# A reordered single-core program: attention and a mixture of experts with new tables of steps, and gate before weight in an expert step

## The chip, the core and the metric

The program runs on one core of one Trainium2 chip. The time is the device time of one execution in microseconds; three runs of the kernel before gave 528.85, 529.96 and 534.11, median 529.96. Engines are named as in the profile: PE is TensorE, ACT ScalarE, DVE VectorE, POOL GpSimd, SP SyncE.

## The reference, cut to what matters

```python
xn = layernorm(x)                                   # x: 4 batches x 1024 tokens x 128
q, k, v = heads(xn @ w_qkv + b_qkv)                 # 16 heads of 8
ctx_g = attend(q[:, :4], k[:, :4], v[:, :4], causal)            # 4 global heads
ctx_l = attend(q[:, 4:], k[:, 4:], v[:, 4:], causal, window 32) # 12 local heads
s = ctx @ w_out + b_out
scores = sigmoid(xn @ gate_w.T)                     # 16 experts, top 2 of 4 groups, top 4 of these
cw = 2.5 * topk_w / topk_w.sum()                    # weight of each expert for each token
y = sum_e cw_e * (silu(xn @ Wg_e.T) * (xn @ Wu_e.T)) @ Wd_e.T + shared expert
out = x + s * silu(xn + y)
```

## The kernel before

Batches are worked on one after the other, in chunks (c = 0, 1) of 512 tokens. The 16 heads form four groups of four: three local groups (g = 0, 1, 2) and the global one (g = 3). One hand-made list of steps per section gives the order of everything: FIRST (before batch 0), BODY (three times, for batches 0 to 2) and LAST (batch 3). A letter of a table takes the next step of a stream: R the attention run, A its operands, X expert steps, P, T and V the preparation, routing and values of the *next* batch, C the context, 0 and 1 the outputs, I the setup. BODY ends with the first six expert steps of the next batch. Every engine walks the same list and does its own part of each step, in that order and with no reordering; semaphores tie the parts together.

The steps that the text names:
- `ln c`, `xT c`, `gate`, `q c`, `k c`: layer norm, transposed x, routing logits (its result `th`, ACT line 926), queries and keys. `q` and `k` are each split into a high and a low part, the low one (`qkl`) by POOL (line 1235); SP then writes both to planes in DRAM.
- `route 0` to `route 6`: choice of experts, small VectorE operations (line 964 and others), which ends with `cw`; `cwT c` transposes it.
- `weights k lo hi`: transposes of expert weights on PE; ACT makes `up_hi` and VectorE `up_lo` for k = 0, 1.
- `strips g`, `pads g half`, `kpads g`: SP's loads of a head group from the planes (2, 4 and 4 DMAs, lines 526, 536 and 546). They wait until the operands that they overwrite have been used; `strips 1` waits until `qfull 0 0` has been copied out of its bank by ACT.
- `max g n`: a product of queries and keys whose row maxima VectorE takes (line 1176, local groups 1178); `maxdone` spreads them (POOL, `maxd`, line 1245), `qfull g c` subtracts them on PE, and ACT copies the result to `qall` (line 929). Group 3 has 48 maximum tiles; `max 3 0` is the first to use the group's strips and pads.
- `score g n`, `pv g n`: scores (ACT takes the exponential, line 936) and their product with the values. `norm`, `fold`, `ctx`, `proj`, `mul`, `outT` end a batch.
- `up c t`: an expert step for a pair of experts (t = 8 the shared one): a tile of the experts' weights (1 matmul, `wrow`), gate and up tiles (3 each). ACT: tanh of the gate (854), a copy `gates` (859) that waits for POOL's multiplication of the step before, and `wrow` (865). POOL multiplies `wrow` (1253); `times c t` multiplies on VectorE (1140) and POOL (1262); `down c t` is the last product.

PSUM has 8 banks. Attention tiles take banks 0 to 2 in turn, expert tiles (and those of preparation) 3 to 5; 6 and 7 are accumulators. A tile waits until its bank's last user has emptied it. `Section.__init__` (line 225) gives out the banks in the list's order.

Of the kernel before, what the change touches and what calls it, by code (L numbers as in the profile page):

```python
# [43 lines left out]
EP = E // 2  # L44
# [97 lines left out]
def expert_steps(c):  # L142
    out = []
    for t in range(NUP + LAG_DOWN):
# [4 lines left out]
        if t >= LAG_DOWN:  # L149
# [1 line left out]
    return out  # L151


FIRST_ORDER = ("IPIPIPPIPIITTPIIPTTTPPVITTPIVIITTIXXXXIVPPPVPPVXXVPXXIXPVPPVXPXXVVXXX")
BODY_ORDER = ("AAXRRAXXAXPARRAXAXRAXAAAAARPRRAXAAAAAAAXAAXRRAARARAARRRRARAAAAAAAAAAAAARAXARAXRRXRPAXRAXAAAARRRA"
              "AARAAAARAXRRARRARRAAAARXARRRRXARAPAARRXRARRRRXRAAPRAXAAXRARXRRRRRARRARRAAPPARXAXRRRPXRRCRRRXXRRR"
              "RRPRTRRPRXRRRRXRRXRTRRRRPXRRTPTXRRXRTXRRRRXXXRRRPRRRRCTRXRRRRRRRRRRRRPTRPXXRXPPPXRRRTRRRPTRXCXVX"
              "CV00XVXVV1X1VXVPV0XXVXV1XXXXX")
LAST_ORDER = ("AXAXARRRXAXARXXRAAAAAAAXAAARAARRRAARXARAARAAAARRRAAXARRAAAAAAAAAAXAAAXAAARXRRRARAXRAAARARRAAAAAA"
              "RXXARARARXRARARARRRAARARAAARARAXAAXAAXARARXAXAARRARRRRRRRRRXRRRRRRXRAAXRRXRXRXRRRXRRRRRCRRRRRXRX"  # L160
              "RCRRRRRXRRRRRRRRRRRRRRRRRRXRXRRRRRXRRRRRRRRRRRRRRRRRRXXRXXCXCXX0X0X1011")
# [42 lines left out]
def batch_steps(more):  # L204
# [14 lines left out]
class Section:  # L219
# [5 lines left out]
    def __init__(self, steps):  # L225
        self.steps, self.place = steps, {}
        self.fills, self.empties = [0] * BANKS, [0] * BANKS
        turns = {ATT: 0, EXP: 0}
        for s in steps:
            if s[0] == "down" and s[2] == 0:  # L230
                self.place[("y", s[1])] = (Y, self.fills[Y], self.empties[Y])
            if s[0] == "z":
                self.add(("z", s[1]), Y, 0)
            if s[0] == "pv" and s[2] == 0:
                self.add(("acc", s[1], 0), ACC, 0)
            if s == ("pv", GLOBAL, CUT):
                self.add(("acc", GLOBAL, 1), ACC, 0)
            if s[0] in ("pv", "down", "norm", "qpads", "z", "z2", "ln", "stats", "pads", "kpads", "maxdone", "ctx", "route", "times",
                        "mul", "strips", "setup", "fill", "ones"):
                continue  # L240
            ahead = s[0] == "max" and s[1] == 0
            ring = EXP if s[0] in ("up", "weights", "xT", "q", "k", "gate") or ahead else ATT
            parts = [s] if s[0] != "up" else [s + (x,) for x in ("weight", "gate", "up") if x != "weight" or s[2] < EP]
            for part in parts:
                self.add(part, ring[turns[ring] % len(ring)], 1)
                turns[ring] += 1
# [45 lines left out]
def build(nc, x, w_qkv, b_qkv, w_out, b_out, gate_w, gate_bias, Wg, Wu, Wd, Ws_g, Ws_u, Ws_d,  # L292
          c32, c16, out):
    with ExitStack() as ctx:
# [109 lines left out]
        k32_loaded = sem("k32_loaded")  # L404
# [156 lines left out]
        def _(pe):  # L561
# [25 lines left out]
            def walk(at):  # L587
                b, opened = at.b, set()
                for s in at.steps:
# [6 lines left out]
                            ins = pe.transpose(ps[:, P * (i - s[2]):P * (i - s[2] + 1)], stage[:, s[1], i, :], ident)  # L596
                        done(at, s, ins)
                    elif kind == "small":
                        pe.wait_ge(k32_loaded, 16)
                        pe.wait_ge(small_loaded, 5 * 16)  # L600
                        pe.wait_ge(small_ready, 1)
                        ps = fill(at, s)
# [166 lines left out]
                    elif kind == "up":  # L769
# [23 lines left out]
                    elif kind == "outT":  # L793
# [551 lines left out]
```

## Time and profile before

| | |
|---|---|
| runs | 528.85, 529.96, 534.11 us |
| the profiled execution | 530.82 us, of it the span 529.0 us |
| granted clock, mean | 0.981 |
| PE / PEld busy | 480.5 us (91%) / 289.0 (55%) |
| DVE / ACT / POOL busy | 340.3 (64%) / 330.3 (62%) / 265.9 us (50%) |
| DMA | 32.37 MB, mean 61 GB/s |

First steps: batch 0 starts (`qfull 0 0` on PE) at 57.72 us, batch 1 at 179.60, batch 2 at 301.92, batch 3 at 421.51. Busy time is the time in which an engine has an instruction in work; PE's instructions overlap, so that its busy time holds small gaps. A busy share is a mean over stages with different limits, so the stages are looked at one by one below. The granted clock is TensorE's: 1.0 is 2.4 GHz, 0.5 is 1.2 GHz.

### The profile page before, as it was taken

How to read it: one execution, taken by the hardware profiler on the slowest of the kernel's cores; microseconds unless marked ns; L12 is line 12 of the kernel's file. 1: busy time of each engine (PE TensorE's matmuls, PEld its weight loads, DVE VectorE, ACT ScalarE, POOL GpSimd, SP SyncE). 2: the span in 40 equal slices, each digit the busy share in tenths (PEclk: the TensorE clock that was granted, in tenths of full speed). 3: DMA queues.
4: the chain of work that ended last, by engine and by line, in shares of the span. 5: the costliest groups of instructions: out<-in, count | busy, mean ns of one | idle time of the engine just before them, and what ended most of it. 6: DMA issues, size and time to landing. Idle time of an engine off the chain costs nothing.

```text
span 529.0 us, 10545 instructions
## 1 busy us (share of the span) xinstructions
PE 480.5 (91%) x3804; PEld 289.0 (55%) x3832; DVE 340.3 (64%) x755; ACT 330.3 (62%) x654; POOL 265.9 (50%) x239
## 2 busy tenths in 40 slices
PE   1969988999999988999999998999999987989995
PEld 0756655555457655555446765555456755544442
DVE  6876464885687555777588474877588532686415
ACT  3456744767957544666957546566967556266972
POOL 3227851265736952155745972155744962016623
PEclk9979998999999999999999999999999999899999
DMA  9256383000350575000360396000260187000001
GB/s 216 80 164 115 58 103 64 1 1 2 124 76 0 165 96 82 1 1 1 93 109 0 91 162 89 2 0 1 82 119 2 48 156 97 2 2 0 1 1 40
DMA packets 144077, 32.37 MB, mean 61 GB/s; under 512 B 120966, under 2 KB 136346, under 8 KB 144026
## 3 DMA queue, kind: packets, MB, share of 16 engines
q1 hardware_dynamic: 143696, 31.41, 30.2%
q8 instruction: 30, 0.49, 0.4%
q10 hardware_dynamic: 330, 0.30, 0.3%
q14 instruction: 21, 0.17, 0.1%
HBM read 22.25 MB, written 9.44 MB: 60 GB/s over the span
## 4 chain that ended last, share of the span: by engine, by line
PE 72%; DVE 9%; ACT 6%; issue 6%; SPq 2%; POOL 2%; DMA 1%; POOLq 1%; DVEq 0%; ACTq 0%
PE bank L791 10%; PE bank L739 7%; PE bank L678 6%; PE bank L572 6%; PE bank L574 6%; PE bank L573 6%; PE bank L708 5%; DVE mxp L1176 4%; PE bank L755 4%; PE bank L779 3%; ACT stage L936 2%; PE bank L690 2%; PE bank L720 2%; PE bank L646 2%; PE bank L662 1%
## 5 line engine op out<-in xcount | busy, mean ns | idle before, releaser
L936 ACT ACTIVATE stage<-bank 128x512 f32<-128x512 f32 (+3 forms) x240 | 112.5, 528 | 62.0 <-PE bank L720 32.2
L1253 POOL TENSOR_TENSOR wrow<-wrow,gates 128x512 f32<-128x512 f32 x64 | 82.1, 1283 | 97.1 <-ACT wrow L865 96.9
L1176 DVE TENSOR_REDUCE mxp<-bank 128x1 f32<-128x512 f32 (+4 forms) x192 | 90.3, 518 | 41.1 <-PE bank L681 32.8
L1262 POOL TENSOR_TENSOR hid<-hid,wrow 128x512 f32<-128x512 f32 x64 | 81.8, 1278 | 37.1 <-DVE hid L1140 31.9
L1140 DVE SCALAR_TENSOR_TENSOR hid<-hid,bank 128x512 f32<-128x512 f32 x72 | 48.7, 680 | 60.0 <-PE bank L574 39.9
L791 PE MATMUL bank<-hid,down_w 128*128 128x512 f32 x144 | 77.8, 629 | 0.0
L854 ACT ACTIVATE hid<-bank 128x512 f32<-128x512 f32 x72 | 43.3, 602 | 51.1 <-PE bank L574 50.9
L1245 POOL TENSOR_TENSOR maxd<-mxp,k 128x512 f16<-128x512 f32 x32 | 33.4, 1048 | 79.7 <-DVE mxp L1176 45.7
L678 PE MATMUL bank<-kall,qpad 128*128 128x512 f16 (+4 forms) x192 | 54.0, 331 | 12.6 <-issue 6.8
L572 PE MATMUL bank<-xh,up_hi 128*128 128x512 f32 x144 | 58.3, 405 | 0.0
L708 PE MATMUL bank<-kpad,kall 128*128 128x512 f16 (+3 forms) x192 | 55.3, 330 | 2.0 <-ACT stage L936 0.6
L574 PE MATMUL bank<-xl,up_hi 128*128 128x512 f32 x144 | 56.7, 394 | 0.0
L573 PE MATMUL bank<-xh,up_lo 128*128 128x512 f32 x144 | 56.5, 392 | 0.0
L1178 DVE TENSOR_REDUCE mxp<-bank 128x8 f32<-128x512 f32 x48 | 31.8, 687 | 23.8 <-PE bank L690 23.4
L708 PEld LDWEIGHTS bank<-kpad,kall 128*128 128x128 f16 x192 | 18.0, 97 | 51.7 <-issue 24.1
L859 ACT ACTIVATE gates<-bank 128x512 f32<-128x512 f32 x72 | 43.2, 600 | 1.6 <-POOL wrow L1253 1.3
L739 PE MATMUL bank<-stage,vg 128*32 128x512 f32 (+3 forms) x384 | 40.5, 498 | 0.0
L678 PEld LDWEIGHTS bank<-kall,qpad 128*128 128x128 f16 x192 | 17.2, 98 | 42.7 <-DVE mxp L1176 23.5
L865 ACT ACTIVATE wrow<-bank 128x512 f32<-128x512 f32 x64 | 39.1, 610 | 0.0
L779 PE MATMUL bank<-cwT,pairsel 128*128 128x512 f32 x64 | 33.7, 526 | 0.8 <-ACT wrow L865 0.7
L572 PEld LDWEIGHTS bank<-xh,up_hi 128*128 128x128 f32 x144 | 27.3, 189 | 9.6 <-issue 3.8
L1123 DVE RECIPROCAL denT<-denT 128x256 f32<-128x256 f32 x16 | 27.8, 1745 | 5.1 <-ACT ctxT L893 5.1
(158 smaller groups left out, 884.4 us busy)
## 6 DMA issues: line engine op xcount, KB each, us to landing
planes<-qkh SPq DMA_DIRECT2D x16, 256.0 KB, 3.1
qtmp<-planes SPq DMA_DIRECT2D x16, 256.0 KB, 3.2
kall<-planes SPq DMA_DIRECT2D x16, 256.0 KB, 3.5
qpad<-planes SPq DMA_DIRECT2D x128, 32.0 KB, 2.9
kpad<-planes SPq DMA_DIRECT2D x48, 64.0 KB, 3.3
xin<-in_L_attn_x_dram SPq DMA_DIRECT2D x4, 512.0 KB, 4.6
planes<-qkl SPq DMA_DIRECT2D x8, 256.0 KB, 3.0
xres<-in_L_attn_x_dram SPq DMA_DIRECT2D x4, 512.0 KB, 4.1
```

Of the source, the lines that this page charges most:

```text
L572: pe.matmul(ps[:], w_hi, x_hi, start=True, stop=False)
L573: pe.matmul(ps[:], w_lo, x_hi, start=False, stop=False)
L574: return pe.matmul(ps[:], w_hi, x_lo, start=False, stop=True)
L678: ins = pe.matmul(ps[:, 0:cols], qpad[:, j, :, :], kall[:, g % 2, CH * c:CH * c + cols], start=True, stop=not last, skip_group_check=True)
L708: ins = pe.matmul(ps[:, 0:cols], kall[:, g % 2, P * j:P * (j + 1)], kpad[:, g % 2, q0 // BLK:(q0 + cols) // BLK, h, :], start=True, stop=n ...
L739: ins = pe.matmul(acc[BLK * h:BLK * (h + 1), q0 - CH * c:q0 - CH * c + cols], vg[:, j, h, :], prob[:, (SCORES_BEFORE[g] + m) % NPROB, 0:cols],
L779: done(at, s + (x,), pe.matmul(ps[:], pairsel[:, t, :], cwT[:, chunk(c)], start=True, stop=True))
L791: pe.matmul(banks[Y][:], down_w[:, t, :], hid[:, i % NHID, :], start=(t == 0), stop=(t == NUP - 1)).then_inc(down_done, 1)
L936: act.activation(prob[:, t % NPROB, 0:cols], ps[:, 0:cols], ACT.Exp).then_inc(freed, 1)
L1176: ins = dve.tensor_reduce(mxp[:, c, j:j + 1], ps[:, 0:cols], AX_X, ALU.max)
L1253: pool.tensor_tensor(row, row, gates[:], ALU.mult).then_inc(gated, 1)
L1262: pool.tensor_tensor(hid[:, i % NHID, :], hid[:, i % NHID, :], wrow[:, (EP * c + t) % NWT, :] if t < EP else gates[:], ALU.mult)\
```

## The change

Three edits. The tables FIRST_ORDER, BODY_ORDER and LAST_ORDER have new values; each holds the same letters as before, so the same steps are done. In an expert step other than the first, the tiles are made in the order gate, weight, up instead of weight, gate, up, and get their banks in that order. TensorE's wait for the 32-bit constants stands at its head instead of in step `small`.

```diff
-FIRST_ORDER = ("IPIPIPPIPIITTPIIPTTTPPVITTPIVIITTIXXXXIVPPPVPPVXXVPXXIXPVPPVXPXXVVXXX")
+FIRST_ORDER = ("PPIPPIPIIPPTITIPITTIIIITTIVPTPVTTPXXVVVXXVIXIVPXPXIXXPVPPPPPVPXVXXXXX")
...
-            parts = [s] if s[0] != "up" else [s + (x,) for x in ("weight", "gate", "up") if x != "weight" or s[2] < EP]
+            parts = [s] if s[0] != "up" else [s + (x,) for x in ("gate", "weight", "up") if x != "weight" or s[2] < EP]
...
                     elif kind == "small":
-                        pe.wait_ge(k32_loaded, 16)
...
-                        for x in ("gate", "up", "weight") if first else ("weight", "gate", "up"):
+                        for x in ("gate", "up", "weight") if first else ("gate", "weight", "up"):
...
+            pe.wait_ge(k32_loaded, 16)
             sections(pe, walk)
```

SP's instructions stand in the same order as before. Lines behind 599 are one lower in the new kernel, up to line 799.

ScalarE (ACT) at the start of the program, before: the constants' setup (lines 819 to 826), both copies of `xT`, then the first `up_hi` and `th`.

```order
L819 ACT_TABLE_LOAD
L819 ACTIVATE kbf<-k 128x128
L822 ACTIVATE kbf<-k 128x448
L823 ACTIVATE kbf<-k 128x64
L822 ACTIVATE kbf<-k 128x448
L823 ACTIVATE kbf<-k 128x64
L824 ACTIVATE repeat<-k 128x512
L826 ACTIVATE pairsel<-k 128x1024
L915 ACTIVATE xT<-bank 128x512 x2
L840 ACTIVATE up_hi<-bank 128x512 x2
L926 ACTIVATE th<-bank 128x128
```

And now:

```order
L915 ACT_TABLE_LOAD
L915 ACTIVATE xT<-bank 128x512
L819 ACTIVATE kbf<-k 128x128
L822 ACTIVATE kbf<-k 128x448
L823 ACTIVATE kbf<-k 128x64
L822 ACTIVATE kbf<-k 128x448
L823 ACTIVATE kbf<-k 128x64
L824 ACTIVATE repeat<-k 128x512
L826 ACTIVATE pairsel<-k 128x1024
L915 ACTIVATE xT<-bank 128x512
L926 ACTIVATE th<-bank 128x128
```

The setup has moved behind the first copy of `xT`, and `q 0` (lines 923 and 924) ahead of the first `up_hi`.

VectorE in the second half of routing, before (`need` and `pre` are route 4, `gt` to `cw` routes 5 and 6):

```order
L964 TENSOR_TENSOR eq<-msk,top 128x128
L964 TENSOR_TENSOR pre<-msk,top 128x8x16
L1029 TENSOR_REDUCE need<-gt 128x8
L964 TENSOR_TENSOR pre<-pre 128x8x16 x4
L964 TENSOR_TENSOR pre<-pre,need 128x8x16
L967 TENSOR_SCALAR pre<-pre 128x8x16
L964 TENSOR_TENSOR eq<-eq,pre 128x128
L964 TENSOR_TENSOR vn_lo<-bank,vn_hi 128x384
L964 TENSOR_TENSOR up_lo<-bank,up_hi 128x512
L964 TENSOR_TENSOR gt<-gt,eq 128x128
L964 TENSOR_TENSOR msk<-sc,gt 128x128
L1046 TENSOR_REDUCE need<-msk 128x8
```

And now:

```order
L964 TENSOR_TENSOR eq<-msk,top 128x128
L964 TENSOR_TENSOR pre<-msk,top 128x8x16
L964 TENSOR_TENSOR up_lo<-bank,up_hi 128x512 x2
L964 TENSOR_TENSOR up_lo<-bank,up_hi 128x128
L1029 TENSOR_REDUCE need<-gt 128x8
L964 TENSOR_TENSOR pre<-pre 128x8x16 x4
L964 TENSOR_TENSOR pre<-pre,need 128x8x16
L967 TENSOR_SCALAR pre<-pre 128x8x16
L964 TENSOR_TENSOR eq<-eq,pre 128x128
L964 TENSOR_TENSOR gt<-gt,eq 128x128
L964 TENSOR_TENSOR msk<-sc,gt 128x128
L1046 TENSOR_REDUCE need<-msk 128x8
```

Two large `up_lo` and a small one stand ahead of route 4, where one large one stood ahead of route 5; `vn_lo` has moved behind route 5.

POOL from the third expert step of the first stage on, before (1253 and 1262 are the two multiplications of a step, `causal` and `foldsel` setup):

```order
L1253 TENSOR_TENSOR wrow<-wrow,gates 128x512
L1262 TENSOR_TENSOR hid<-hid,wrow 128x512
L1245 TENSOR_TENSOR maxd<-mxp,k 128x512
L1253 TENSOR_TENSOR wrow<-wrow,gates 128x512
L1208 MEMSET causal 32x32
L1208 MEMSET causal 32x64
L1208 MEMSET causal 32x96
L1213 CAST causal<-k 32x32 x4
L1217 COPY foldsel<-k 128x32 x2
L1262 TENSOR_TENSOR hid<-hid,wrow 128x512
L1253 TENSOR_TENSOR wrow<-wrow,gates 128x512
L1245 TENSOR_TENSOR maxd<-mxp,k 128x512
```

And now:

```order
L1253 TENSOR_TENSOR wrow<-wrow,gates 128x512
L1262 TENSOR_TENSOR hid<-hid,wrow 128x512
L1253 TENSOR_TENSOR wrow<-wrow,gates 128x512
L1208 MEMSET causal 32x32
L1208 MEMSET causal 32x64
L1208 MEMSET causal 32x96
L1213 CAST causal<-k 32x32 x4
L1217 COPY foldsel<-k 128x32 x2
L1262 TENSOR_TENSOR hid<-hid,wrow 128x512
L1245 TENSOR_TENSOR maxd<-mxp,k 128x512 x2
L1253 TENSOR_TENSOR wrow<-wrow,gates 128x512
```

Both `maxd` of group 0 stand together, ahead of the fifth `wrow`; before, the first stood ahead of the fourth `wrow` and the second behind the fifth.

TensorE in BODY, from `max 3 12` (416 columns) on, before; 791 is `down`, 715 and 720 a score of group 2:

```order
L678 MATMUL bank<-kall,qpad 128x416
L681 MATMUL bank<-kbf 128x32
L678 MATMUL bank<-kall,qpad 128x448
L681 MATMUL bank<-kbf 128x32
L791 MATMUL bank<-hid,down_w 128x512
L678 MATMUL bank<-kall,qpad 128x480
L681 MATMUL bank<-kbf 128x32
L715 MATMUL bank<-kbf 128x512
L720 MATMUL bank<-qall,kpad 128x64 x8
L678 MATMUL bank<-kall,qpad 128x512
L681 MATMUL bank<-kbf 128x32
L791 MATMUL bank<-hid,down_w 128x512
```

And now:

```order
L677 MATMUL bank<-kall,qpad 128x416
L680 MATMUL bank<-kbf 128x32
L790 MATMUL bank<-hid,down_w 128x512
L677 MATMUL bank<-kall,qpad 128x448
L680 MATMUL bank<-kbf 128x32
L677 MATMUL bank<-kall,qpad 128x480
L680 MATMUL bank<-kbf 128x32
L677 MATMUL bank<-kall,qpad 128x512
L680 MATMUL bank<-kbf 128x32
L790 MATMUL bank<-hid,down_w 128x512
L714 MATMUL bank<-kbf 128x512
```

`down 0 7` stands one tile earlier, and the score between the last two maxima has gone to the other three behind `down 0 8`.

## Rows read from the trace of the kernel before

**Rows 1.** Stretches: us, PE, PEld, DVE, ACT, POOL busy (count), clock, DMA, GB/s.
```profile
0.00:57.72 57.72, 39.27 (x191) 31.13 (x194) 40.85 (x116) 28.47 (x51) 25.63 (x36) 0.94 0.55 132
57.72:85.11 27.39, 23.48 (x321) 15.98 (x324) 13.14 (x37) 16.65 (x31) 17.02 (x15) 1.00 0.69 105
85.11:93.75 8.64, 8.35 (x74) 4.34 (x75) 7.46 (x21) 2.59 (x6) 1.05 (x1) 0.80 0.09 9
...
179.60:206.92 27.32, 23.31 (x321) 16.07 (x324) 12.99 (x37) 15.93 (x30) 15.32 (x13) 1.00 0.81 141
206.92:216.04 9.12, 8.82 (x73) 4.33 (x75) 7.37 (x21) 2.54 (x6) 1.05 (x1) 0.81 0.08 9
216.04:242.38 26.34, 25.28 (x222) 14.35 (x221) 21.50 (x44) 17.80 (x39) 12.05 (x10) 1.00 0.00 1
242.38:281.99 39.61, 39.21 (x240) 19.88 (x240) 27.34 (x66) 30.46 (x63) 20.16 (x18) 1.00 0.32 68
...
301.92:327.54 25.62, 23.34 (x322) 16.01 (x325) 13.01 (x37) 15.45 (x29) 15.33 (x13) 1.00 0.83 148
327.54:335.64 8.10, 7.67 (x74) 3.95 (x75) 7.37 (x21) 2.89 (x7) 1.05 (x1) 1.00 0.13 14
...
449.41:486.92 37.51, 34.66 (x288) 18.25 (x289) 27.88 (x59) 17.84 (x38) 11.92 (x10) 0.95 0.01 2
```

**Rows 2.** Timeline of SyncE's queue, batch 1: start us, us, line, operation.
```profile
180.90 0.34 SPq L526 DMA_DIRECT2D qtmp<-planes  x1
...
197.13 4.02 SPq L546 DMA_DIRECT2D kpad<-planes  x4
...
202.37 4.36 SPq L536 DMA_DIRECT2D qpad<-planes  x8
```

**Rows 3.** Timeline of TensorE, batch 1; in brackets the idle time before, releaser.
```profile
206.92 0.18 PE L678 MATMUL bank<-kall,qpad 128*128 128x32 f16 x1 [1.45 <-issue]
```

**Rows 4.** Timeline of VectorE, first stage.
```profile
4.42 1.76 DVE L1105 MEMSET kpad<- 128x2048 uint32 x1 [0.38 <-issue]
...
33.39 0.68 DVE L964 TENSOR_TENSOR up_lo<-bank,up_hi 128x512 fp32r<-128x512 f32 x1
...
35.79 0.29 DVE L1053 SCALAR_TENSOR_TENSOR cw<-msk,wsum 128x128 f32<-128x128 f32 x1
...
44.39 1.28 DVE L1178 TENSOR_REDUCE mxp<-bank 128x8 f32<-128x512 f32 x2
```

**Rows 5.** The view of the line that loads the first x.
```profile
DMA to landing us min/median/max: 4.7/4.7/4.7
```

**Rows 6.** Timeline of ScalarE, first stage.
```profile
4.50 0.31 ACT L819 ACTIVATE kbf<-k 128x128 bf16<-128x128 f32 x1
...
6.46 1.04 ACT L826 ACTIVATE pairsel<-k 128x1024 fp32r<-128x1024 f32 x1
13.71 0.60 ACT L915 ACTIVATE xT<-bank 128x512 f32<-128x512 f32 x1 [6.20 <-PE bank L614]
...
19.89 0.28 ACT L926 ACTIVATE th<-bank 128x128 f32<-128x128 f32 x1 [2.63 <-PE bank L646]
```

**Rows 7.** VectorE's additions of routing: count, ns min/median/max, first and last start us.
```profile
L964 DVE TENSOR_TENSOR pre<-pre x4: 281/292/1153, 29.7 to 30.8; 128x128 f32<-128x128 f32 x4
...
L964 DVE TENSOR_TENSOR msk<-msk,gm x1: 1278/1278/1278, 26.5 to 26.5; 128x128 f32<-128x128 f32 x1
```

**Rows 8.** Timeline of POOL, first stage.
```profile
30.67 1.15 POOL L1235 TENSOR_TENSOR qkl<-sT,qkh 128x512 f16<-128x512 f32 x1 [1.77 <-ACT qkh L924]
40.82 1.29 POOL L1253 TENSOR_TENSOR wrow<-wrow,gates 128x512 f32<-128x512 f32 x1 [9.00 <-ACT wrow L865]
...
47.86 1.29 POOL L1253 TENSOR_TENSOR wrow<-wrow,gates 128x512 f32<-128x512 f32 x1 [1.44 <-ACT wrow L865]
...
56.72 1.26 POOL L1253 TENSOR_TENSOR wrow<-wrow,gates 128x512 f32<-128x512 f32 x1
```

**Rows 9.** Timeline of SyncE's queue, the first strips of batch 0.
```profile
59.66 0.34 SPq L526 DMA_DIRECT2D qtmp<-planes  x1
```

More of the change, by code:

```diff
@@ L151, in expert_steps @@
     return out
-FIRST_ORDER = ("IPIPIPPIPIITTPIIPTTTPPVITTPIVIITTIXXXXIVPPPVPPVXXVPXXIXPVPPVXPXXVVXXX")
[L155 to L161, printed above, removed]
+FIRST_ORDER = ("PPIPPIPIIPPTITIPITTIIIITTIVPTPVTTPXXVVVXXVIXIVPXPXIXXPVPPPPPVPXVXXXXX")
+BODY_ORDER = ("AAAXRRRXAPRXXXAAAAAAAXRXAAARARPRAAXAAAAARXAXRRRRRAAAAARRRAAAAAAAARAAAAAAXAAAXRRRRXAPRAXXAAAARRRA"
+              "AAAARAAXRRARARARRRARAAAXXRARRRARRAPRAAXARRRRRXRRAAPAXAAXRRRRRXAAARRRRRRAAXRAPPAXRRPRXRRRXRXRTRRR"
+              "RRPRRTPRRRRRXRRTXRRRXXRPRRRRXRXRRRRRPPTRCTRXTXRRRRXRXCRRPRXTPRRRRPPRRRRRRRRXRXXPRRRRRXRTTRPCXXVX"
+              "V0XVC0VXVXVXV1V1VXXP0X1VXXXXX")
+LAST_ORDER = ("AAXXARRRRRAXAXXAARRXAARAAAARAXAXAAARRARAARRXAAAARARRAAAAAAAAAAAAAAXAAAXARAXRRRAAXARARRARARRAAAAA"
+              "RXAXARAARARARARRRRAARRAAAARXAAXARAXARXARAXAAAXAARRRRRRRXRRRXRRRRRRRRAAXRXRXRRXRRRRXXRRRRRRRRRRRX"
+              "RCRRRXRRRRRRCRRRRXRRRRRRRRXRRRRRRXRRXRRRRRRRRRRRRRRRRRXRXXX0XCCX0X1X011")
 FIRST_EXPERTS = expert_steps(0) + [("z", 0), ("z2", 0)]
```

## The prediction

> **What bounds the kernel now.** I read the page's busy shares, then the table by stretches [rows 1], then SyncE's and TensorE's timelines, then the start of the program on every engine. Batch 1 stands for batches 0 to 2; the marks are the first TensorE instruction of a step. The reader is to see four kinds of stretch in [rows 1].
>
> From the first query-bias tile of a batch to the first global maximum tile (`max 3 0`): 27.39 us in batch 0, 27.32 in batch 1, 25.62 in batch 2. TensorE has about 23.3 of work there. SyncE is what ends it: it issues strips, pads and k pads of three head groups without a pause, from 180.90 to beyond 202.37 [rows 2], and `max 3 0`, which needs the first half of the third group's pads, starts at 206.92 after 1.45 us of waiting for nothing but a transfer [rows 3]. The length of this stretch is that of 34 issues, counted from the first, `strips 1`: 30 of them took the 21.5 us between these two rows.
>
> Then 9.12 us (batch 1) or 8.10 (batch 2) to the batch's step `up 1 0`. The granted clock is 0.81 in one and 1.00 in the other: TensorE is at 1.2 GHz for part of the first, after the waits above.
>
> Then 26.34 us up to the routing logits (`gate`), with VectorE 21.50 busy, since 32 maximum tiles and four `times` go through it: VectorE and its hand-overs bound it. In the last batch this and the stretch before it together take 37.51 us, VectorE 27.88 busy.
>
> Then 39.61 us with TensorE 39.21 busy: only TensorE bounds it, and no order of the same steps shortens it. The first stage, 57.72 us with TensorE 39.27 busy, is a chain over VectorE and POOL (below).
>
> **The change, part by part.** No instruction's size changes. What moves is which waits are covered.
>
> *Waits and the order in a step.* The wait for the 32-bit constants moves to TensorE's head; they are used later anyway, so 0. Gate before weight: TensorE makes the gate tile one matmul earlier in a step and asks for the bank of the previous gate, which ScalarE gives back before the weight's. TensorE is 39.21 of 39.61 busy where steps are dense, so this is worth 0 there; in the first stage it is inside the next sum.
>
> *Batch starts.* SyncE's rows stay the same, word for word. Its 34 issues start when `qfull 0 0` has been evacuated, and that step stays first. So moving scores, downs and maxima within this stretch changes how much TensorE waits and not where `max 3 0` starts: 0, three times and in the last batch. If SyncE had to wait for a later maximum, it would cost; the nearest, the first half of pads 2 behind `max 1 1`, keeps its place in BODY.
>
> *From `max 3 0` to `up 1 0`.* `down 0 7` moves ahead of `max 3 13`, and the four scores of group 2 stand together. VectorE is 7.37 of 9.12 busy, so at most 1.7 per batch is there to gain. A score no longer waits between two maxima; I take 0.4, nearer to nothing, since all maxima keep their place: 3 x 0.4 = -1.2 for batches 0 to 2 and 0 for the last; ends 0 and -5.1.
>
> *From `up 1 0` to `gate`.* VectorE idles 4.84 of 26.34 in each body batch, and 9.63 of 37.51 in the last. Scores, `times` and `pv` change places by one to three steps, the maxima hardly. I take 0, with ends of 1.5 us per batch either way, a third of that idle time.
>
> *The first stage.* Here real things move.
> 1. VectorE's memset of `kpad` (1.76, [rows 4]) leaves the place ahead of the statistics. x is issued at 0.73 and lands 4.7 later [rows 5], so they start near 5.5 instead of 6.1, when that memset is over: -0.6. But it now stands between the two halves of the layer norm, and the second half ends 1.76 + 0.38 - 0.6 = 1.5 later, near 15.
> 2. ScalarE's setup of constants, seven activations from 4.50 to 7.50 [rows 6], ran while x was loaded. Now it stands between the copies of `xT 0` (its end, 14.31 before, is 0.6 earlier) and `xT 1`: 13.7 + 3.0 + 0.6 = 17.3. `gate` needs both and starts near 18.0, so `th` is at 21.4 instead of 19.89 [rows 6]: +1.5.
> 3. Routing on VectorE took 19.89 to 36.08, 16.2 us [rows 4, 6]. The change puts two more large `up_lo` into it, 2 x 0.68 [rows 4], and ScalarE evacuates `q 0` ahead of the first `up_hi` that VectorE then waits for, about 1.1. Two routing operations of about 0.29 took 1.28 and 1.15 [rows 7], the second exactly beside POOL's `qkl` of 30.67 to 31.82 [rows 8]. POOL now has `q 0` and `k 0` early and `q 1` and `k 1` only after routing's longest parts, so I take off both stretches, 0.99 + 0.86. Routing ends at 21.4 + 16.2 + 1.4 + 1.1 - 1.85 = 38.25: +2.2.
> 4. From there to POOL's first `wrow` it is 40.82 - 36.08 = 4.74 [rows 4, 8]; so that starts at 43.0.
> 5. POOL then runs to the end of its fifth `wrow`, 57.98, in 17.16 us, with 1.44 idle [rows 8]. The idle time goes, since it starts later; a second `maxd` (1.04) comes ahead of this `wrow`. 43.0 + 17.16 - 1.44 + 1.04 = 59.8: +1.8. ScalarE's `gates` of the sixth step waits for it, and the copy of `qfull 0 0` stands behind that; so `strips 1` is issued near 61.5 to 61.7 instead of 59.66 [rows 9]: **+2.0**.
>
> What is late next: `k 1` ends on POOL near 41, not at 31.8 [rows 8]. The first maximum was reduced 12.6 later, at 44.39 [rows 4], so now near 53.7; POOL reaches its `maxd` near 56.7, so 3 us are left. Ends of this term: 0 (the two later parts absorbed by POOL and TensorE) and +3.9.
>
> Whose stretch it was: VectorE's addition took 1.15 while POOL read two inputs, 0.29 otherwise, in one and the same line [rows 7]. The Trainium skill (SBUF — State Buffer, "Who interferes with whom") says that a VectorE instruction with two SBUF inputs and a GpSimd instruction that reads SBUF exclude each other for a whole instruction. The trace agrees. By that rule the 1.85 goes, as taken; without it, with the stretches kept, the sum is 1.85 higher.
>
> **Sum.** The profiled execution took 530.82 us (span 529.0 and 1.8 around it). 530.82 + 2.0 - 1.2 = 531.6. It lies 0.86 above the median of the runs, 529.96; on that scale the forecast is **530.8 us**.
>
> **Rivals.**
> *Slower: VectorE's stretch loses.* Place: `up 1 0` to `gate`, four times. For it: the same 26.3 us three times over [rows 1], so whatever the order does there it does in each batch; more scores stand directly behind one another in the ring of three banks that the maxima use too. Against it: VectorE's work is the same 21.5. Price: 1.5 x 4 = 6 us, 536.8. It decides from 1.1 us per batch.
> *Faster: the same stretch gains.* `times 1 0` now fills VectorE while TensorE makes two scores. Price 1.6 x 4 = 6.4, 524.4.
> *Batches start as batch 2 does.* It needed 25.62 + 8.10 = 33.72 against 36.44 in batch 1 and 36.03 in batch 0: shorter k-pad issues (4.02 in batch 1, [rows 2]) and no low clock. The table of orders does not move these issues, so it would be luck: -2.7 -2.3 and as much in the last batch, minus what is forecast, near 524.5.
> *The first stage loses nothing:* POOL and TensorE take up the 2.0: 528.8.
> *The stretches stay* (the page's rule is not what lengthened them, or another POOL operation lands there): 532.6.
> *The change does nothing it says:* if transfers were not what the order was short of, times stay at 529 to 531; this is within the forecast.
>
> **Numbers.** Chances: forecast 0.45, stretches stay 0.10, first stage loses nothing 0.12, slower 0.16, faster stretch 0.12, starts as batch 2 0.05. A measurement of this kernel tells about 1%, 5.3 us, from no change. Below 524.7 lie the two faster cases, 0.17; above 535.3 the slower one, 0.16; between them 0.67. The range leaves out the far halves of both: 523.5 to 537.0. The forecast's own range is 528.5 to 533.5.
>
> **What would show it.** Right: `th` near 21.4, the routing weights `cw` near 38.3, POOL's first `wrow` near 43.0, `strips 1` near 61.6; SyncE without gaps from there and `max 3 0` about 25.5 us behind it; VectorE near 21.5 busy in 26.3 us from `up 1 0` to `gate`. Wrong: `cw` at 36 or at 41; a wait of SyncE inside its 34 issues; a stretch to `gate` of less than 25.2 or more than 27.4; another number of stretches with granted clock 0.8.

## The result, and the profile after

Twenty runs of the changed kernel gave a median of 533.75 us (530.96 to 539.28), twenty of the kernel before 530.99 us (525.70 to 534.11). The ratio is 1.007, 95% interval 1.0047 to 1.0092: about 3.7 us slower by the ratio, 2.8 us by the medians. That is within the range on record (523.5 to 537.0), 3 us above the forecast of 530.8 and just outside the forecast's own range (528.5 to 533.5). The forecast was a loss of 0.8 us, so the size of the change was missed by a factor of some four.

The profiled execution of the changed kernel took 530.96 us (span 529.2), the lowest of its twenty, while that of before, 530.82, was a middling one. So the two spans are nearly equal, and the loss has to be looked for in stretches. The table by stretches, columns as in [rows 1] (a stretch, length, then busy us and count of PE, PEld, DVE, ACT and POOL, granted clock, DMA share, GB/s):

```profile
0.00:62.62 62.62, 38.31 (x192) 30.06 (x194) 40.43 (x116) 28.82 (x53) 28.06 (x38) 0.92 0.51 121
62.62:88.75 26.13, 22.86 (x321) 15.87 (x324) 12.08 (x37) 14.29 (x27) 14.65 (x13) 1.00 0.72 110
88.75:96.66 7.91, 7.54 (x73) 3.99 (x75) 7.39 (x20) 3.62 (x8) 1.05 (x1) 1.00 0.13 13
182.54:208.41 25.87, 22.84 (x321) 15.87 (x324) 12.34 (x37) 14.58 (x28) 15.30 (x13) 1.00 0.84 144
208.41:216.32 7.91, 7.55 (x73) 3.99 (x75) 7.39 (x20) 3.72 (x8) 1.05 (x1) 1.00 0.13 13
216.32:242.65 26.33, 24.85 (x221) 14.54 (x220) 20.86 (x44) 17.39 (x38) 12.70 (x10) 1.00 0.01 2
302.19:328.64 26.45, 22.83 (x321) 15.88 (x324) 12.06 (x37) 15.57 (x29) 15.31 (x13) 1.00 0.83 143
328.64:336.55 7.91, 7.55 (x74) 4.00 (x75) 7.40 (x20) 2.74 (x7) 1.05 (x1) 1.00 0.15 15
450.18:487.91 37.73, 35.30 (x292) 19.06 (x294) 28.23 (x59) 19.91 (x43) 12.30 (x10) 0.95 0.02 3
```

The first row is 62.62 us long against 57.72 in [rows 1]: 4.9 us lost before batch 0 starts. Later starts lie closer: `qfull 0 0` of batch 1 at 182.54 (179.60 before), of batch 2 at 302.19 (301.92), of batch 3 at 422.69 (421.51). This execution was a lucky one there: from the first of these starts to the last it took 360.1 us, and four other kernels with the same batches (they differ from the changed one in the first table alone) took 363.5 to 367.3. The stretch from `max 3 0` to `up 1 0` is 7.91 us three times, with granted clock 1.00, where [rows 1] show 8.64 and 9.12 at 0.80 and 0.81, and 8.10 at 1.00. Beside the passage of 8.10, at the same clock, the new order gains 0.2. The low clock is not the old table's doing: body_last_new (below) has the new BODY table and took 8.74 us at 0.80 in batch 0, and a_old_first, which has it too, shows a granted clock of 0.81 from 83.2 to 92.0 us. The stretch behind `up 1 0` (26.33 against 26.34, VectorE 20.86 busy against 21.50) is unchanged; it ends here just behind the last maximum tile, since the new table puts `gate` 3.4 us later.

The first stage in rows that answer to [rows 4], [rows 6] and [rows 9], of ScalarE, VectorE and SyncE's queue (start and length in us; in brackets the idle time before and what ended it):

```profile
21.90 0.28 ACT L926 ACTIVATE th<-bank 128x128 f32<-128x128 f32 x1 [4.55 <-PE bank L645]
...
39.25 0.29 DVE L1053 SCALAR_TENSOR_TENSOR cw<-msk,wsum 128x128 f32<-128x128 f32 x1
...
54.63 0.69 DVE L1178 TENSOR_REDUCE mxp<-bank 128x8 f32<-128x512 f32 x1 [2.19 <-PE bank L689]
...
63.91 0.34 SPq L526 DMA_DIRECT2D qtmp<-planes  x1
```

POOL's row, which answers to [rows 8], dense from its first `wrow` on but for 0.43 us ahead of the fifth:

```profile
44.23 1.30 POOL L1253 TENSOR_TENSOR wrow<-wrow,gates 128x512 f32<-128x512 f32 x1 [1.94 <-ACT wrow L865]
...
59.92 1.30 POOL L1253 TENSOR_TENSOR wrow<-wrow,gates 128x512 f32<-128x512 f32 x1 [0.43 <-ACT wrow L865]
```

`th` is 2.0 later than before, `cw` 3.5, POOL's first `wrow` 3.4, `strips 1` 4.25. The chain of waits of the same stretch (start, us, what) goes another way than through POOL's row, through the pads and TensorE:

```profile
39.98 1.17 POOL qkl L1235
41.16 0.52 SPq L517
...
44.31 4.47 DMA planes<-qkl
48.80 0.34 SPq L526
...
53.55 2.35 DMA qpad<-planes
55.91 0.05 issue
55.96 0.39 PE bank L683
```

And TensorE waits for these pads in front of the first maxima; in brackets idle time and releaser:

```profile
51.49 1.02 PE L790 MATMUL bank<-hid,down_w 128*128 128x512 f32 x2
54.20 0.39 PE L689 MATMUL bank<-kall,qpad 128*128 128x32 f16 x8 [1.70 <-DMA qpad<-planes]
...
55.96 0.39 PE L683 MATMUL bank<-kbf 128*128 128x512 bf16 x1 [0.47 <-DMA qpad<-planes]
```

The reader is to see two ways that meet near 60 us: routing, `cw`, POOL's row of multiplications; and `k 1`, planes, strips, pads, maxima, then the fifth and sixth expert step on TensorE. In this execution the second came last. ScalarE's copy of `qfull 0 0`, which `strips 1` waits for, had been waiting for TensorE, with POOL's fifth `wrow` over at 61.22:

```profile
63.24 1.08 ACT L929 ACTIVATE qall<-bank 128x512 f16<-128x512 f32 x2 [0.64 <-PE bank L662]
```

### The profile page after: what moved, and what is told of

The parts are those of the page before. It is cut to its first block, busy times and chain, and to the rows that moved or that the text cites. A ratio compares the mean times of both kernels' runs of the same rounds, so it can differ in the third digit from the quotient of the medians.

```text
span 529.2 us, 10542 instructions
## 1 busy us (share of the span) xinstructions
PE 474.1 (90%) x3805; PEld 287.0 (54%) x3832; DVE 339.9 (64%) x755; ACT 328.5 (62%) x654; POOL 267.4 (51%) x239
## 4 chain that ended last, share of the span: by engine, by line
PE 72%; DVE 6%; SPq 6%; issue 5%; ACT 5%; DMA 4%; POOL 1%; DVEq 1%; POOLq 0%; ACTq 0%
PE bank L790 10%; PE bank L738 7%; PE bank L572 7%; PE bank L707 6%; PE bank L574 6%; PE bank L573 6%; PE bank L677 5%; PE bank L754 4%; DVE mxp L1176 4%; SPq L536 3%; PE bank L778 2%; PE bank L689 2%; ACT stage L936 2%; PE bank L719 2%; DMA kall<-planes 2%
## 5 line engine op out<-in xcount | busy, mean ns | idle before, releaser
L790 PE MATMUL bank<-hid,down_w 128*128 128x512 f32 x144 | 76.7, 618 | 0.0
L572 PE MATMUL bank<-xh,up_hi 128*128 128x512 f32 x144 | 66.4, 461 | 0.4 <-DVE hid L1140 0.3
L677 PE MATMUL bank<-kall,qpad 128*128 128x512 f16 (+4 forms) x192 | 51.8, 321 | 10.7 <-issue 3.5
L738 PE MATMUL bank<-stage,vg 128*32 128x512 f32 (+3 forms) x384 | 39.4, 496 | 0.0
L1235 POOL TENSOR_TENSOR qkl<-sT,qkh 128x512 f16<-128x512 f32 x16 | 18.9, 1182 | 38.0 <-ACT qkh L924 38.0
L929 ACT ACTIVATE qall<-bank 128x512 f16<-128x512 f32 x32 | 18.1, 596 | 23.4 <-PE bank L662 23.4
```

The costliest lines, as they stand in the source:

```text
L572: pe.matmul(ps[:], w_hi, x_hi, start=True, stop=False)
L677: ins = pe.matmul(ps[:, 0:cols], qpad[:, j, :, :], kall[:, g % 2, CH * c:CH * c + cols], start=True, stop=not last, skip_group_check=True)
L738: ins = pe.matmul(acc[BLK * h:BLK * (h + 1), q0 - CH * c:q0 - CH * c + cols], vg[:, j, h, :], prob[:, (SCORES_BEFORE[g] + m) % NPROB, 0:cols],
L790: pe.matmul(banks[Y][:], down_w[:, t, :], hid[:, i % NHID, :], start=(t == 0), stop=(t == NUP - 1)).then_inc(down_done, 1)
```

## The experiments

Each ratio is to the kernel before, with its 95% interval; "strips 1" and "max 3 0" are starts in batch 0 of the profiled execution, one for each kernel.

| kernel | median us | ratio | strips 1 | max 3 0 |
|---|---|---|---|---|
| before | 530.99 | 1 | 59.66 | 85.11 |
| changed | 533.75 | 1.007 (1.0047 to 1.0092) | 63.91 | 88.75 |
| first_new | 533.83 | 1.006 (1.0027 to 1.0093) | 63.23 | 88.13 |
| gate_first | 528.60 | 0.9952 (0.9922 to 0.9981) | 57.89 | 83.13 |
| body_last_new | 530.22 | 0.9999 (0.9966 to 1.0032) | 58.86 | 83.40 |
| a_old_first | 530.07 | 1.0006 (0.9978 to 1.0035) | 57.92 | 83.24 |
| a_weight_first | 536.28 | 1.0098 (1.0064 to 1.0132) | 64.43 | 89.07 |
| a_k1_early | 532.75 | 1.0057 (1.0027 to 1.0088) | 64.15 | 89.23 |
| a_setup_early | 534.48 | 1.0072 (1.0042 to 1.0103) | 62.93 | 88.32 |
| a_warm | 533.64 | 1.0059 (1.0028 to 1.009) | 63.30 | 88.58 |
| a_warm_k1 | 532.93 | 1.0054 (1.0025 to 1.0084) | 61.63 | 87.11 |
| kpads_late | 524.30 | 0.989 (0.9845 to 0.9935) | 58.84 | 82.96 |
| kp_gate | 521.38 | 0.9846 (0.9807 to 0.9885) | 57.91 | 82.08 |
| best | 519.70 | 0.9801 (0.9762 to 0.984) | 57.79 | 80.43 |

### The parts of the change, one at a time

**first_new**, the kernel before with the new first table and the moved wait of TensorE:

```diff
-FIRST_ORDER = ("IPIPIPPIPIITTPIIPTTTPPVITTPIVIITTIXXXXIVPPPVPPVXXVPXXIXPVPPVXPXXVVXXX")
+FIRST_ORDER = ("PPIPPIPIIPPTITIPITTIIIITTIVPTPVTTPXXVVVXXVIXIVPXPXIXXPVPPPPPVPXVXXXXX")
...
-                        pe.wait_ge(k32_loaded, 16)
...
+            pe.wait_ge(k32_loaded, 16)
```

> The kernel before with the new FIRST_ORDER alone (and the wait for the 32-bit constants at TensorE's head); BODY, LAST and the order of tiles as before. Theory A (the whole loss of the change is made in the first stage and the start of batch 0, through the later k 1, the planes and the first maxima): strips 1 issued near 63.9 instead of 59.66 us, max 3 0 of batch 0 between 88.5 and 89.5 instead of 85.11, and the time 3 to 4.5 us above the kernel before, since nothing behind it gives anything back. Rival B (the first stage's loss is absorbed later and BODY and LAST cost what the change costs): within 1 us of the kernel before.

Measured 1.006, 3.2 us: the whole loss, as theory A had it. `strips 1` came at 63.23 and `max 3 0` at 88.13, each a little earlier than it said.

**gate_first**, the kernel before with the order of tiles alone:

```diff
-            parts = [s] if s[0] != "up" else [s + (x,) for x in ("weight", "gate", "up") if x != "weight" or s[2] < EP]
+            parts = [s] if s[0] != "up" else [s + (x,) for x in ("gate", "weight", "up") if x != "weight" or s[2] < EP]
...
-                        for x in ("gate", "up", "weight") if first else ("weight", "gate", "up"):
+                        for x in ("gate", "up", "weight") if first else ("gate", "weight", "up"):
```

> The kernel before with the one change of the order gate, weight, up in an expert step, in its banks too. All tables as before. Theory A: 0, within 0.7 us of the kernel before, since TensorE is 39.2 of 39.6 us busy where steps are dense and elsewhere SyncE or VectorE sets the end. Rival B: the weight tile, one matmul later in each step, makes ScalarE's wrow and POOL's multiplication later, and the DVE-bound stretches from up 1 0 to gate lengthen from 26.3 to some 27 us: 2 to 3 us slower.

Neither: 2.5 us faster (interval 1.0 to 4.1 of 530). In the first stage it is about 1 us: `strips 1` at 57.89 against 58.86 and 58.84 in the two profiles with the same first table and weight first (59.66 in the kernel before). POOL waited 0.54 us for its third `wrow` where it had waited 1.44, and 1.42 in body_last_new. From `qfull 0 0` of batch 0 to that of the last batch it took 364.7 us, no less than before (363.8), so the trace places no more than that 1 us.

**body_last_new**, the kernel before with the other two tables:

```diff
-BODY_ORDER = ("AAXRRAXXAXPARRAXAXRAXAAAAARPRRAXAAAAAAAXAAXRRAARARAARRRRARAAAAAAAAAAAAARAXARAXRRXRPAXRAXAAAARRRA"
+BODY_ORDER = ("AAAXRRRXAPRXXXAAAAAAAXRXAAARARPRAAXAAAAARXAXRRRRRAAAAARRRAAAAAAAARAAAAAAXAAAXRRRRXAPRAXXAAAARRRA"
...
-LAST_ORDER = ("AXAXARRRXAXARXXRAAAAAAAXAAARAARRRAAXARAARAAAARRRAAXARRAAAAAAAAAAXAAAXAAARXRRRARAXRAAAARARRAAAAAA"
+LAST_ORDER = ("AAXXARRRRRAXAXXAARRXAARAAAARAXAXAAARRARAARRXAAAARARRAAAAAAAAAAAAAAXAAAXARAXRRRAAXARARRARARRAAAAA"
```

> The kernel before with the new BODY_ORDER and LAST_ORDER alone; the first stage as before. Theory A: up 1 0 comes 0.3 to 1.2 us earlier behind max 3 0 in each of three batches (8.6 and 9.1 us before, 7.9 in the changed kernel), all else the same: 1 to 3 us below the kernel before. Rival B (the new tables cost what the change costs): 2 to 4 us above it.

0.9999: both theories miss, and the prediction's -1.2 for these tables is not seen; the interval, some 1.8 us either way, can't exclude it. `max 3 0` to `up 1 0` took 8.74, 7.91 and 8.24 us.

**a_old_first** and **a_weight_first** undo one part of the change each:

```diff
-FIRST_ORDER = ("PPIPPIPIIPPTITIPITTIIIITTIVPTPVTTPXXVVVXXVIXIVPXPXIXXPVPPPPPVPXVXXXXX")
+FIRST_ORDER = ("IPIPIPPIPIITTPIIPTTTPPVITTPIVIITTIXXXXIVPPPVPPVXXVPXXIXPVPPVXPXXVVXXX")
```

> The changed kernel with the old FIRST_ORDER; new BODY, LAST and gate-first stay. Theory A (FIRST_ORDER alone makes the loss, and the other two parts add up as when each was done alone: gate-first 2.5 us faster, BODY and LAST 0): about 2.5 us below the kernel before, ratio 0.995, strips 1 near 58 us. Rival B (the parts disturb each other in the batches, since the tables were made for each other): no better than the kernel before, within 1 us.

Measured 1.0006, so undoing the first table gives back 1.007 - 1.0006 = 0.0064, 3.4 us. The moved wait stayed here, so the loss is the table's. Theory A's additivity is not seen: 0.9952 was expected from gate-first, and rival B's number came out.

```diff
-                        for x in ("gate", "up", "weight") if first else ("gate", "weight", "up"):
+                        for x in ("gate", "up", "weight") if first else ("weight", "gate", "up"):
```

> The changed kernel with the tiles of an expert step in the old order weight, gate, up. Theory A (gate-first gains some 2.5 us wherever it stands): 2.5 us above the changed kernel, about 6 above the kernel before. Rival B (it gains in the first stage through an earlier gates and wrow only where POOL waits for them; in the new first stage POOL is fed without a gap from 44 us on): equal to the changed kernel within 1 us, about 3 above the kernel before.

Measured 1.0098, 1.5 us above the changed kernel (the intervals overlap): between the two theories. In the trace `strips 1` is 0.5 later, less than the 1 us of the old first table.

### Which way through the first stage decides

**a_k1_early** takes `q 1` and `k 1` forward (the rest of the table is the same):

```diff
-FIRST_ORDER = ("PPIPPIPIIPPTITIPITTIIIITTIVPTPVTT...")
+FIRST_ORDER = ("PPIPPIPIIPPTITIPIPPTTIIIITTIVTVTT...")
```

> The changed kernel with the steps q 1 and k 1 moved directly behind k 0 in FIRST_ORDER, ahead of the weights of experts 1 and routing's second half. Theory A1 (the way k 1, planes, strips, pads, first maxima sets the start of batch 0): planes written near 38 instead of 45.2 us, max 0 2 at 51 to 53 instead of 55.96, strips 1 some 2 us earlier than 63.91 and the time 2 us below the changed kernel. Rival B1 (POOL's row of multiplications from its first wrow at 44.2 us on, without a gap, sets it): max 0 2 earlier all the same, but strips 1 within 1 us of 63.9, or later if POOL's two qkl now stand beside VectorE's routing and stretch an instruction there to about 1.2 us each, as 27.09 and 27.11 did.

SyncE's strips of batch 0's first group moved from 48.80 to 38.84, and `strips 1` did not move:

```profile
31.75 0.52 SPq L517 DMA_DIRECT2D planes<-qkh  x1
...
38.84 0.35 SPq L526 DMA_DIRECT2D qtmp<-planes  x1
...
64.15 0.34 SPq L526 DMA_DIRECT2D qtmp<-planes  x1
```

That is B1's number, but it does not show B1, nor does it refute A1. The maxima hardly moved either (the first was reduced at 54.72, 54.63 in the changed kernel), because the steps ahead of them on TensorE came late, and so did POOL's first `wrow`, at 45.72 against 44.23. Between `cw` and that `wrow` TensorE had half the clock in this execution; the first row is the changed kernel's, the second this one's, columns as above:

```profile
39.60:45.10 5.50, 4.61 (x26) 3.59 (x26) 3.79 (x7) 3.93 (x8) 3.19 (x3) 1.00 0.47 149
39.60:45.10 5.50, 5.50 (x19) 4.07 (x19) 2.65 (x5) 2.39 (x5) 0.00 (x0) 0.50 0.83 144
```

The clock was at half from 35.0 to 45.2 us. The eight transposes of `cwT` there took 1.91 us instead of 1.04. With a first `wrow` 1.5 later POOL's row became the last of the two ways (its fifth `wrow` ended at 62.47, and ScalarE's `gates` waited 1.28 for it), while the other had become shorter. How much of the 1.5 us is the order's and how much the clock's, this one profile can't tell.

**a_setup_early** puts ScalarE's setup ahead of both copies of `xT`:

```diff
-FIRST_ORDER = ("PPIPPIPIIPPTITIPITTIIIITTIVPTPVTT...")
+FIRST_ORDER = ("PPIPIPPIIPPTITIPITTIIIITTIVPTPVTT...")
```

> The changed kernel with ScalarE's setup of constants back ahead of both copies of xT. If the prediction's step 2 was right (the setup between the copies delays the gate by 1.5 us and everything down to POOL's first wrow with it): gate near 16.7 instead of 18.30, cw 1.5 earlier than 39.25, first wrow near 42.7 and strips 1 1.5 us earlier, the time 1.5 us below the changed kernel. If k 1 and the planes set it and are not moved by it: 0.

The second copy of `xT` starts at 16.25 instead of 16.77, but `gate` stays at 18.19:

```profile
15.10 1.12 PE L613 MATMUL bank<-k,xin 128*128 128x128 f32 x4 [1.85 <-DVE xin L967]
16.15 0.29 PE L602 MATMUL bank<-k,vectors 20*128 20x20 f32 x1
16.27 0.58 PE L603 MATMUL bank<-gb_row,ones_row 1*128 1x16 f32 x2
18.19 3.57 PE L645 MATMUL bank<-turned,xT 128*128 128x16 f32 x16 [1.33 <-DVE gb L1156]
```

So the setup was worth nothing at `gate` but the 0.1 by which this whole start lies earlier (the memset of `kpad` too), and the prediction's step 2 had the wrong cause. The layer norm's second half (1.85 of idle TensorE behind the moved memset) and step `small`, whose `gb` on VectorE now comes behind the casts of `xT 1`, hold it. `strips 1`, at 62.93, lies 1.0 earlier than in the changed kernel and the time no lower: that much the landmark varies.

**a_warm** takes two groups of weight transposes back ahead of `gate`:

```diff
-FIRST_ORDER = ("PPIPPIPIIPPTITIPITTIIIITTIVPTPVTT...")
+FIRST_ORDER = ("PPIPPIPIIIIPPTTPITTIIIITTIVPTPVTT...")
```

> The changed kernel with the first two transposes of experts' weights (weights 0 0 4 and 0 4 8) moved ahead of gate, where they stood before the change; they fill TensorE's 1.3 us of waiting for gb. In all profiles of the new FIRST_ORDER gate's 16 matmuls took 3.57 us, in five of six of the old one 1.86 to 2.10, all at a granted clock shown as 1.00. Theory W (what TensorE did just ahead of gate sets its pace): gate takes about 2 us, th and cw come 0.5 to 1.5 us earlier, strips 1 with them, and the time is 0.5 to 1.5 us below the changed kernel. Rival (another cause, such as the place of the sixteen matmuls behind xT 1): gate still 3.4 to 3.6 us, and later by what the transposes take, about 0.6 us; time the same or 1 us above.

Half of each. `gate` still took 3.43 us, so theory W's cause is not it. But the transposes filled TensorE's wait, `gate` started at 18.35 all the same, and two of the large `up_lo` stood ahead of routing instead of within it: `cw` at 37.10, POOL's first `wrow` at 42.04, 2.2 earlier, and `strips 1` only 0.6 earlier. POOL came to wait for the fifth step, which stood behind the maxima on TensorE:

```profile
42.04 1.28 POOL L1253 TENSOR_TENSOR wrow<-wrow,gates 128x512 f32<-128x512 f32 x1 [1.94 <-ACT wrow L865]
...
59.30 1.29 POOL L1253 TENSOR_TENSOR wrow<-wrow,gates 128x512 f32<-128x512 f32 x1 [1.36 <-ACT wrow L865]
```

**a_warm_k1** makes both moves:

```diff
-FIRST_ORDER = ("PPIPPIPIIPPTITIPITTIIIITTIVPTPVTT...")
+FIRST_ORDER = ("PPIPPIPIIIIPPTTPIPPTTIIIITTIVTVTT...")
```

> The changed kernel with both moves in FIRST_ORDER: weights 0 0 4 and 0 4 8 ahead of gate, and q 1 and k 1 behind k 0. The first alone brought POOL's first wrow from 44.23 to 42.04 but strips 1 only from 63.91 to 63.30, the second alone planes from 41.16 to 31.75 but strips 1 from 63.91 to 64.15. Theory T (two ways lie within 1 us of each other, POOL's row of multiplications and k 1 to the first maxima; each hides the other's gain): together strips 1 at 61.5 to 62.3 and 1.5 to 2 us below the changed kernel, ratio to the kernel before about 1.003. Rival U (a third thing, such as TensorE's own row of steps from max 0 0 on, holds it): strips 1 at 63.2 or later, ratio 1.006 or more.

`strips 1` came at 61.63, inside theory T's 61.5 to 62.3, though each move alone gave 0.6 and -0.2. Against the profile of the changed kernel that is 2.3 earlier, with POOL's first `wrow` at 43.41 and the planes at 29.59. It is the earliest of the seven profiles with the new table (62.93 to 64.43 the others); the granted clock was at half for 3.4 us from 33.9 on, in the changed kernel for 10.2 us from 28.3 on, so not all of the 2.3 need be the order's. Free of that is this distance: from the end of POOL's fifth `wrow` to `strips 1` it is 1.68 us in the kernel before (57.98 to 59.66), in a_k1_early (62.47 to 64.15) and here (59.95 to 61.63), and 1.68 or 1.69 in all nine profiles where the pads are early; it is 2.69 in the changed kernel (61.22 to 63.91) and 2.40 to 2.71 in all five where they are late. That second way costs 1.0 us in the changed kernel, and 0.4 more if POOL's wait of 0.43 for the fifth step is counted. The time, 1.0054, can't tell T's 1.003 from U's 1.006: what is shown is the landmark, not the microseconds of the whole.

### Is SyncE's issuing the bound of a batch's start?

**kpads_late** lets SyncE issue a group's k pads behind the next group's strips and first pads:

```diff
     ahead = [("strips", g + 1), ("pads", g + 1, 0)] if 0 < g < GLOBAL else []
+    made, ahead = (ahead, made) if ahead else (made, ahead)
```

> The kernel before with SyncE's k pads of group 1 and 2 issued behind the strips and first pads of the next group instead of ahead of them; the tables are as before. If SyncE's issuing sets the start of the global maxima, as the prediction took it: the four k pads of group 2 (4.0 us in batch 1, 2 to 3 in batch 2) no longer stand ahead of the pads that max 3 0 needs, which starts 2 to 4 us earlier in every batch as long as the scores of group 2 don't come to wait; 5 to 10 us less in all. If the transfers' throughput or their landing sets it, or TensorE has no room left in this stretch (23.3 of 27.3 us busy): max 3 0 within 1 us of where it was, and the time within 1 us of the kernel before. If the scores come to wait for the late k pads: slower by 1 to 4 us, with a wait of TensorE at line 720.

Measured 0.989, 5.8 us faster. SyncE's queue in batch 1, with one line added ahead of these (line 537 is the pads, 547 the k pads), answers to [rows 2]; behind it, SyncE's own waits from 178 to 206 us (in total, times, longest):

```profile
178.20 0.34 SPq L527 DMA_DIRECT2D qtmp<-planes  x1
...
184.93 0.43 SPq L527 DMA_DIRECT2D kall<-planes  x1
187.27 2.06 SPq L537 DMA_DIRECT2D qpad<-planes  x4
189.37 2.66 SPq L547 DMA_DIRECT2D kpad<-planes  x4
...
195.51 2.62 SPq L537 DMA_DIRECT2D qpad<-planes  x4
```

```profile
SPq L537 <- DVE mxp L1179: 1.9, 1, 1.9
```

From `strips 1` to `max 3 0` it is now 24.14 us in batch 1 against 26.02, and `max 3 0` follows the work before it without a gap (it waited 1.45 in [rows 3]). So what stands in SyncE's queue ahead of the third group's pads was the bound. Moving the k pads moves their transfers too; but the 16 DMA engines were not full while the k pads of group 2 were issued in the kernel before (busy share 0.60 from 197 to 202 us), which speaks for the issuing and not the throughput. No run changed one without the other. Of the 4.0 us taken out of its way 1.9 were gained, since SyncE now waits 1.9 us at 185.4 for `max 1 1` on VectorE, ahead of the pads of group 2. It is the wait that the prediction named as the nearest.

**kp_gate** and **best** look for the fastest sum. The first is kpads_late with gate first; the second is the changed kernel with the old first table and late k pads.

> The kernel before with k pads issued behind the next group's strips and first pads, and with gate first in an expert step; all tables as before. If the two gains add up (5.8 and 2.5 us): ratio to the kernel before near 0.984, about 522 us. If gate-first's gain was chance or lies in the same waits: 0.989, about 524.5.

> The changed kernel with the old FIRST_ORDER and the k pads late. If the new BODY and LAST cost 2 to 3 us when gate stands first (0.9952 without them, 1.0006 with them): 2 to 3 us above the run with k pads late and gate first alone, near 525. If that difference was chance: equal to it within 1 us.

0.9846 and 0.9801. kp_gate adds up as the sum of its parts. best fits neither of its two expectations: it came 1.7 us below kp_gate, neither 2 to 3 above it nor within 1 us. best is the fastest, 10.6 us below the kernel before and 14 below the changed one, and it beats kp_gate by 0.0045, which is inside the two intervals. With k pads early, BODY and LAST had cost 0.0054 beside gate-first (1.0006 against 0.9952); with k pads late they cost nothing. One difference is as large as the other, in opposite directions, and either may be chance; that stays open.

## Why the prediction was nearly right

**The first stage: the step that was mis-sized.** The prediction gave +2.0; alone, this table cost 3.2 us (first_new), and undoing it gave back 3.4. At `strips 1` it is +4.25 between the two profiles. By the prediction's own steps:
- Step 1 and 2: `gate` was to start near 18.0 and `th` at 21.4; 18.30 and 21.90. The number was close by luck: not ScalarE's setup but the later layer norm and `gb` hold it (a_setup_early).
- Step 3: routing was to end at 38.25, the end of `cw`; it ended at 39.54 (39.25 + 0.29), 0.5 of it from `th`. Of the other 0.8, 0.4 is VectorE's wait for ScalarE's first `up_hi`, 1.51 instead of 1.1. The other 0.4 is in the stretches:

```profile
25.23 0.69 DVE L964 TENSOR_TENSOR up_lo<-bank,up_hi 128x512 fp32r<-128x512 f32 x1 [1.51 <-ACT up_hi L840]
```

  Both stretched additions of [rows 7] went, as was taken, but POOL's `qkl` of `k 0` hit another operation of routing:

```profile
27.09 1.15 POOL L1235 TENSOR_TENSOR qkl<-sT,qkh 128x512 f16<-128x512 f32 x1 [1.22 <-ACT qkh L924]
```

```profile
27.11 1.28 DVE L964 TENSOR_TENSOR cmp<-cmp 128x128 f32<-128x128 f32 x1
```

  The first row is POOL's, the second VectorE's; alone this operation takes 0.29 (kernel before, 22.88), so 0.99 was lost again. The prediction had overlooked a third stretched operation of the kernel before, and that one went too, 0.62 of it:

```profile
24.06 0.91 DVE L964 TENSOR_TENSOR cmp<-cmp,k 128x128 f32<-128x128 f32 x1
```

  So the stretches gave back 0.99 + 0.86 + 0.62 - 0.99 = 1.5 of the 1.85 taken. In a_setup_early it was `cw` itself, 1.20 beside a `qkl` of 38.19, against 0.29. The rule that the prediction took from the Trainium skill (SBUF — State Buffer, "Who interferes with whom") held each time; taking off both stretches without asking where the moved operations land was a mistake of 0.4 us in the net. Of the rival "the stretches stay", priced at 1.85, a fifth came true.
- Steps 4 and 5: from the end of `cw` to POOL's first `wrow` 4.69 against 4.74, from there to the end of the fifth 17.0 against 16.8: right.
- "What is late next: 3 us are left" was wrong. The first maximum was reduced at 54.63, not 53.7, and TensorE, which does its steps in order, stood still for it with the fifth and sixth expert steps behind it; POOL's `maxd` was not the place where the slack ended. It cost the 1.0 us that stands between the profiles with late and with early pads, and, as far as one profile shows it, POOL's 0.43. This is the way that the prediction did not have.

**The profile that the sum began from was not typical in its first stage.** Its `strips 1` at 59.66 is the latest of seven profiles with the old first table; the other six lie at 57.79 to 58.86. TensorE reached its full pace at 28.1 us in that execution and at 16.3 to 17.4 in the six others (last section). Against those with the same order of tiles the new table's first stage is 4.4 us (63.23 against 58.86, weight first) to 6.0 us (63.91 against 57.9, gate first) longer up to `strips 1`, more than the +3.9 of the term's upper end. Part of that is TensorE's early pace: with the same order of tiles and a late full pace in both, first_new is 3.6 us later than the kernel before (63.23 against 59.66), and the kernel before 0.8 later than the two others of its order. The times show 3.2 and 3.4 us; where the rest is given back is not settled, since the batches differ by more than that from one execution to the next (360.1 to 367.3 us in five kernels with the same batches).

**Batch starts: right.** SyncE's queue sets them (kpads_late), and from `strips 1` to `max 3 0` it took 24.84 against 25.45 where 25.5 was forecast.

**`max 3 0` to `up 1 0`:** 0.2 per batch where 0.4 was taken, and the time of body_last_new does not show it. **`up 1 0` to `gate`:** 0, as forecast; `max 3 47` follows `up 1 0` by 26.2 us, 26.1 before. Taken to the word, the prediction's sign of being wrong (more than 27.4 us up to `gate`) is met, 29.7 us, because the table puts `gate` itself later; the maxima that bound the stretch end when they did. Another sign of being wrong is met as well: no passage of the changed kernel's profile shows the clock 0.8, where two did before. The slower rival, placed in this stretch, was wrong in its place, though the sign came out on its side.

**Gate first:** taken at 0 because TensorE is dense; 2.5 us faster in the kernel before, 1.5 in the changed one (1.0098 against 1.007, within the intervals). The term left out the first stage, where the copy `gates` and the multiplications behind it wait for that tile; that is worth 1 us, and the rest of the 2.5 is not placed.

**Luck.** Taken alone the parts give 3.2 for the first table, 0 for the other two and -2.5 for the tiles, 0.7 in all, next to the forecast's 0.8; together they cost 3.7. The 3.0 between may be an interaction, whose cause no run shows, or noise: each of the four ratios has an interval of 1.2 to 1.8 us either way. And the range held because it was made wide for the stretch from `up 1 0` to `gate`, which lost nothing.

## What to carry to other kernels

Where two ways through a stage end within a microsecond of each other, moving one shows little: price the stage by both, and test with both moved. Before reading a landmark of one profile as the order's doing, compare the granted clock of the stretch ahead of it. For every moved operation, look where the operation that excludes it on the other engine will stand, not only at the place it leaves. And where a queue's issues are the bound, look at their order first: here one line gave 5.8 us, and three new tables gave none.

## What the runs showed of the hardware

**TensorE's early pace differs between executions, and the granted clock does not show it.** The same sixteen matmuls of `gate` in the kernel before and in gate_first, where the work ahead of them is the same:

```profile
16.42 3.43 PE L646 MATMUL bank<-turned,xT 128*128 128x16 f32 x16
```

```profile
16.43 2.10 PE L646 MATMUL bank<-turned,xT 128*128 128x16 f32 x16
```

They follow one another by 213 ns in the first; in the second by 213 up to 16.9 us, where the trace has its first record of the granted clock, and by 112 from there. In the kernel before that first record stands at 28.1. The profile's clock column says 1.00 for both stretches, but 213 against 112 is close to the ratio of 2.4 to 1.2 GHz, so these matmuls ran at the lower level up to that first record. Of seven profiles with the old first table six have the first record at 16.3 to 17.4 us, and all seven with the new one at 24.8 to 27.1, where TensorE has idle time of 1.85 and 1.3 us between `xT 0` and `gate`; that this is the cause was not shown. Transposes in the second of these gaps did not change it (a_warm, 26.0). The Trainium skill (TensorE: Matmul & The Clock Gate, "What's actually happening") says that the point of this transition varies from run to run and that it costs under 1% of a kernel; the profiles agree that it varies (16.3 to 28.1 us with the same first table), and the only cost that they show, 0.8 us at `strips 1` (59.66 against 58.86 and 58.84), is 0.15% of the kernel. With the new order it was late each time. What it costs in the whole was not tried alone.

**One VectorE instruction beside one POOL instruction lasts about as long as POOL's:** 0.42 became 1.35 for `wqk_lo` beside `xl` (1.27, changed kernel), 0.29 became 1.28 and 1.20 beside `qkl` (1.15 and 1.16). All of these read two tiles in SBUF.

**A pad's issue takes SyncE's queue 0.5 to 0.9 us, a k pad's 0.7 to 1.1, in the mean of a group:** over the fourteen profiles eight pads took 4.14 to 7.49 us and four k pads 2.66 to 4.35, with the same instructions each time.

**Half the clock lengthened a chain that runs over several engines:** eight small transposes took 1.91 us instead of 1.04 at a granted clock of 0.50 (a_k1_early), on the way from `cw` to POOL's row.
